# Gated cross-attention with LoRA feed-forward: Q and K of all heads in a phase of their own, by a Strassen scheme, and the rest of the attention in a second phase

## The reference

```
h   = layernorm(x);  xn = rmsnorm(h) * ln_weight
q   = xn @ w_q.T   k = ctx @ w_k.T   v = ctx @ w_v.T        # 1024 x 4096 each, 512 deep
score = q . k + position_bias[head];  masked softmax over 128 keys
attn  = h + (probs . v) @ w_out.T                            # 1024 x 512, 4096 deep
x1  = x + tanh(g_xattn) * attn
y   = layernorm(x1)
out = x1 + tanh(g_ffn) * (y @ base_W.T + base_b + LoRA with a top-8 router)
```

## Time and profile before

| | us |
|---|---|
| median of 3 runs | 947.47 (946.6 to 947.58) |
| the profiled execution | 948.59 |
| its span, first to last instruction | 946.8 |
| PE busy | 920.2 |
| DVE, ACT, POOL busy | 559.4, 437.3, 404.4 |
| DMA | 46.55 MB, mean 49 GB/s |

### The profile page before, as it was taken

The page is one execution under the profiler, slowest core; times in us unless marked ns, Lnnn a source line. Parts: engine busy times, 40 slices in busy tenths (PEclk is TensorE's granted clock), DMA queues, the critical chain, the costliest instruction groups (busy, mean ns, idle before and its releaser), DMA issues.

```text
span 946.8 us, 15495 instructions
## 1 busy us (share of the span) xinstructions
PE 920.2 (97%) x5408; PEld 813.3 (86%) x5408; DVE 559.4 (59%) x953; ACT 437.3 (46%) x1074; POOL 404.4 (43%) x270
## 2 busy tenths in 40 slices
PE   4899999999999999999999999999999999999898
PEld 3788888888888888888888888888888888888787
DVE  7857555556555565556555564556555565657974
ACT  4665444544445454444545354445444454544410
POOL 5345253534445253534534254434525354443432
PEclk9899999999999999999999999999999999999899
DMA  8013020110202020010202020020202020021001
GB/s 289 22 61 136 5 71 23 52 40 3 91 3 91 3 69 25 27 64 3 91 3 91 3 69 22 11 83 3 91 3 87 7 64 28 3 83 56 1 23 67
DMA packets 18929, 46.55 MB, mean 49 GB/s; under 512 B 2528, under 2 KB 7264, under 8 KB 18400
## 3 DMA queue, kind: packets, MB, share of 16 engines
q1 hardware_dynamic: 18912, 46.33, 14.3%
HBM read 44.22 MB, written 2.10 MB: 49 GB/s over the span
## 4 chain that ended last, share of the span: by engine, by line
PE 89%; DVE 6%; ACT 2%; issue 1%; POOL 1%; DMA 1%; SPq 0%; ACTq 0%; DVEq 0%; POOLq 0%
PE QP L1006 6%; PE Ob L1006 6%; PE Vb L1008 6%; PE Vb L1007 6%; PE Vb L1006 6%; PE Ob L1007 6%; PE Ob L1008 6%; PE Kb L1006 6%; PE Kb L1007 6%; PE Kb L1008 6%; PE QP L1008 6%; PE QP L1007 6%; PE Ab L1088 4%; PE Sb L1076 4%; PE QP L1066 3%; PE Sb L1077 2%
## 5 line engine op out<-in xcount | busy, mean ns | idle before, releaser
L336 POOL TENSOR_TENSOR bms<-bm,small_s 128x512 f32<-128x512 f32 x63 | 96.7, 1535 | 208.8 <-ACT small_s L468 208.8
L483 ACT ACTIVATE p_exp<-s_sb,negmax 128x128 f32<-128x128 f32 x256 | 99.8, 391 | 138.2 <-DVE negmax L704 138.2
L1006 PE MATMUL Vb<-v_hi,cT_lo 128*128 128x256 f32 x504 | 143.6, 285 | 9.9 <-DVE cT_lo L638 9.9
L1008 PE MATMUL Vb<-v_hi,cT_hi 128*128 128x256 f32 x504 | 143.8, 285 | 0.0
L1007 PE MATMUL Vb<-v_lo,cT_hi 128*128 128x256 f32 x504 | 143.8, 285 | 0.0
L302 POOL TENSOR_TENSOR qk_lo<-qk_raw,qk_hi 128x1024 fp32r<-128x1024 f32 x32 | 76.8, 2400 | 130.0 <-ACT qk_hi L422 130.0
L422 ACT ACTIVATE P_hl<-QP 128x512 fp32r<-128x512 f32 x64 | 38.4, 599 | 196.9 <-PE QP L1066 196.9
L736 DVE TENSOR_TENSOR acc<-Ob,acc 128x512 f32<-128x512 f32 x120 | 82.2, 685 | 64.7 <-PE Ob L1008 64.7
L1006 PEld LDWEIGHTS Vb<-v_hi,cT_lo 128*128 128x128 f32 x504 | 97.6, 194 | 14.9 <-DVE cT_lo L638 9.9
L1006 PE MATMUL QP<-xT_hi,qk_lo 128*128 128x512 f32 x256 | 104.6, 409 | 0.0
L702 DVE TENSOR_TENSOR s_sb<-Sb,bms 128x512 f32<-128x512 f32 x64 | 44.3, 692 | 101.6 <-POOL bms L336 101.3
(11 more groups left out here) (204 smaller groups left out, 2141.8 us busy)
## 6 DMA issues: line engine op xcount, KB each, us to landing
qk_raw<-wqk SPq DMA_DIRECT2D x32, 512.0 KB, 4.7
v_raw<-wv SPq DMA_DIRECT2D x16, 512.0 KB, 6.0
o_raw<-wo SPq DMA_DIRECT2D x16, 512.0 KB, 3.5
bias_sb<-bias SPq DMA_DIRECT2D x32, 64.0 KB, 1.8
qk_raw<-x SPq DMA_DIRECT2D x2, 1024.0 KB, 5.1
stage<-ctxT SPq DMA_DIRECT2D x4, 256.0 KB, 4.9
acc<-x SPq DMA_DIRECT2D x4, 256.0 KB, 6.8
acc<-x SPq DMA_DIRECT2D x1, 1024.0 KB, 9.9
```

Of the source, the lines that this page charges most:

```text
L336: pool.tensor_tensor(bms[:, :, :], bm[:, :, :], small_s[:, :, :], ALU.add).then_inc(bms_done, 1)
L483: last = act.activation(p_exp[:, i, :], s_sb[:, i, :], ACT.Exp, bias=negmax[:, i:i + 1], accum_out=rowsum[:, i:i + 1])
L1006: pe.matmul(dst, w_lo, m_hi, start=start, stop=False)
L1008: return pe.matmul(dst, w_hi, m_hi, start=False, stop=stop)
```

## The change

Q and K leave the unit's step. They are computed first, in 32 jobs of their own: 16 for K of the head pairs, then 16 for Q. A job is one 2 by 2 block product: the weights of two heads by the two halves of the depth, times the transposed tokens by the same halves and the two halves of the batches. Strassen's scheme (in the Winograd form) makes the four result blocks from seven block products instead of eight. Each product is 2 chunks of the depth by 3 matmuls of 512 columns, so a job is 42 matmuls where the same results took 48.

The seven products need sums. Four sums of weight blocks are made in every job by DVE, 256 wide (`weight_sums`). Four sums of token blocks are made once for the context and once for x. The results are put together partly in PSUM: one bank of `X` takes M1, M6, M7 and M4 one on top of the other, and ACT copies out what stands there after the first three (`snapshot_1` to `snapshot_3`), while DVE adds `Y` (M2) and `Z` (M5, M3) to these. The finished blocks are split into `hi` and `lo` and stored in DRAM (`qk_units`), 512 KB each, four in a job.

The second phase has a unit's scores first, on Q and K that SP has loaded (1 MB a unit, two buffers), then V, output tile, transposes, V, output tile, probabilities times V. Its first output tile goes to `Kb`, the second to `Ob`. The split of the output weights moves from DVE to POOL. What concerns x (norms, transposes, splits) lies between jobs 2 and 16. The feed-forward part is the same work in nearly the same order.

```diff
@@ host: order of the weight blocks, the new tensor in DRAM @@
+    def head_pairs(w):
+        a = heads(w, 1).reshape(G, 2, P, 2, 2 * DH)
+        return np.stack([a[:, 0, :, 0], a[:, 0, :, 1], a[:, 1, :, 1], a[:, 1, :, 0]], axis=2)
...
+    args.append(nc.dram_tensor("qk_units", (UNITS, P, 2, 2 * TH), F32, kind="Internal").ap())
@@ SyncE @@
+            def store(i, n):
+                sp.wait_ge(unit_lo_done[i], n + 1)
+                sp.dma_start(qk_units[4 * (n % G) + i, :, n // G, :], f32(unit_out[:, i, :])).then_inc(st[i], 16)
...
+            for n in range(JOBS + 1):
+                if n + 2 < JOBS:
+                    load_w(n + 2)
...
+                    store(R22, n - 1)
+                if n < JOBS:
+                    store(R11, n)
+                if n > 0:
+                    store(R21, n - 1)
+                    store(R12, n - 1)
+            def load_unit(t, parity):
+                sp.wait_ge(scores_done, t - 1)
+                sp.dma_start(f32(qk[:, parity, :, :]), qk_units[t, :, :, :]).then_inc(ld_qk[parity], 16)
@@ GpSimd, first phase @@
+            def c22_lo(n):
+                pool.wait_ge(unit_hi_done[R22], n + 1)
+                pool.tensor_tensor(unit_half(R22, n, 1), by_batch(C22[:, :]), f32(unit_half(R22, n, 0)),
+                                   ALU.subtract).then_inc(unit_lo_done[R22], 1)
...
+            def first_weights_lo(n):
+                pool.wait_ge(w1_hi, n + 1)
+                pool.tensor_tensor(w_lo[:, n % 2, 0:5, :], w_raw[:, n % 2, 0:5, :], f32(w_hi[:, n % 2, 0:5, :]),
+                                   ALU.subtract).then_inc(w1_lo, 1)
...
+            for n in range(JOBS + 1):
+                if n > 0:
+                    c22_lo(n - 1)
+                if 0 < n < JOBS - 1:
+                    first_weights_lo(n + 1)
+                if n in (3, 4):
+                    rms_root(n - 3)
+                if n in (2, 3):
+                    layernorm_root(n - 2)
+                if n + 1 < JOBS:
+                    last_weights_lo(n + 1)
@@ ScalarE, first phase @@
+            def first_weights_hi(n):
+                act.wait_ge(ld_w[n % 2], 16 * (n // 2 + 1))
+                act.wait_ge(s_add, 4 * n + 3)
+                reached(act, m_done[7], n - 1)
+                high(w_hi[:, n % 2, 0:5, :], w_raw[:, n % 2, 0:5, :], w1_hi)
+            def last_weights_hi(n):
+                act.wait_ge(s_add, 4 * n + 4)
+                reached(act, m_done[3], n - 1)
+                high(w_hi[:, n % 2, 5:7, :], w_raw[:, n % 2, 5:7, :], w2_hi)
+            def snapshot_1(n):
+                act.wait_ge(m_done[1], n + 1)
+                reached(act, c11_done, n)
+                high(U1[:, :], X[n % 2], u1_done)
...
+            for n in range(1, JOBS + 1):
+                snapshot_3(n - 1)
...
+                snapshot_1(n)
+                c22_hi(n - 1)
+                if n + 1 < JOBS:
+                    first_weights_hi(n + 1)
...
+                c11_hi(n)
+                c21_hi(n - 1)
...
+                snapshot_2(n)
...
+                if n + 1 < JOBS:
+                    last_weights_hi(n + 1)
+                c12_hi(n - 1)
...
+                if 5 <= n < 5 + B:
+                    x_evict(n - 5)
+                if n == 9:
+                    x_block_hi(B11)
+                if n == 10:
+                    x_block_hi(B21)
+                if n == 13:
+                    x_block_hi(B22)
+                if n == G - 1:
+                    x_sum_hi(T2, 6)
@@ VectorE, first phase @@
+            def weight_sums(n):
+                w = w_raw[:, n % 2, :, :]
+                dve.wait_ge(ld_w[n % 2], 16 * (n // 2 + 1))
+                dve.tensor_tensor(w[:, S1, :], w[:, A21, :], w[:, A22, :], ALU.add).then_inc(s_add, 1)
+                dve.tensor_tensor(w[:, S3, :], w[:, A11, :], w[:, A21, :], ALU.subtract).then_inc(s_add, 1)
+                dve.wait_ge(s_add, 4 * n + 1)
+                dve.tensor_tensor(w[:, S2, :], w[:, S1, :], w[:, A11, :], ALU.subtract).then_inc(s_add, 1)
+                dve.wait_ge(s_add, 4 * n + 3)
+                dve.tensor_tensor(w[:, S4, :], w[:, A12, :], w[:, S2, :], ALU.subtract).then_inc(s_add, 1)
...
+            def c11(n):
+                dve.wait_ge(m_done[2], n + 1)
+                dve.wait_ge(u1_done, n + 1)
+                reached(dve, unit_lo_done[R11], n)
+                dve.tensor_tensor(C11[:, :], Y, U1[:, :], ALU.add).then_inc(c11_done, 1)
...
+            def unit_lo(i, n, src):
+                dve.wait_ge(unit_hi_done[i], n + 1)
+                low(unit_half(i, n, 1), by_batch(src), unit_half(i, n, 0), unit_lo_done[i])
...
+            for n in range(1, JOBS + 1):
+                c22(n - 1)
...
+                if n + 1 < JOBS:
+                    weight_sums(n + 1)
+                c11(n)
+                unit_lo(R11, n, C11[:, :])
+                if n == G:
+                    x_sum_lo(T2)
+                    x_sum_lo(T1)
+                unit_lo(R21, n - 1, X[(n - 1) % 2])
+                if n == 2:
+                    layernorm_stats(0)
+                if n == 3:
+                    rms_stats(0)
+                    layernorm_stats(1)
+                if n == 4:
+                    rms_stats(1)
...
+                if 4 <= n < 4 + B:
+                    normed(n - 4)
+                if n == 10:
+                    x_block_lo(B11)
+                if n == 11:
+                    x_block_lo(B21)
+                if n == 14:
+                    x_block_lo(B22)
+                    x_sum(T1, B12, B11, 0)
+                    x_sum(T3, B22, B12, 1)
+                if n == 15:
+                    x_sum(T2, B22, B11, 2)
+                    x_sum(T4, B21, B22, 3)
+                if n == 18:
+                    gated_base_b()
+                    router_constants()
+                c12(n - 1)
+                unit_lo(R12, n - 1, C12[:, :])
@@ TensorE @@
+            def blocks(bank, n, a, m_hi, m_lo, fresh, done):
+                for c in range(2):
+                    cols = slice(c * DH, (c + 1) * DH)
+                    hi, lo, first = w_hi[:, n % 2, a, cols], w_lo[:, n % 2, a, cols], fresh and c == 0
+                    pe.matmul(bank, lo, m_hi[:, c, :], start=first, stop=False, skip_group_check=not fresh)
+                    pe.matmul(bank, hi, m_lo[:, c, :], start=False, stop=False, skip_group_check=not fresh)
+                    last = pe.matmul(bank, hi, m_hi[:, c, :], start=False, stop=c == 1, skip_group_check=not fresh)
+                last.then_inc(done, 1)
...
+            def m1(n):
+                pe.wait_ge(w1_lo, n + 1)
+                kept_ready(n, B11)
+                reached(pe, unit_lo_done[R21], n - 1)
+                blocks(X[n % 2], n, A11, *kept(n, B11), True, m_done[1])
+            def m2(n):
+                kept_ready(n, B21)
+                reached(pe, c11_done, n)
+                blocks(Y, n, A12, *kept(n, B21), True, m_done[2])
+            def m3(n):
+                pe.wait_ge(w2_lo, n + 1)
+                kept_ready(n, B22)
+                pe.wait_ge(c22_done, n + 1)
+                blocks(Z[n % 2], n, S4, *kept(n, B22), False, m_done[3])
+            def m4(n):
+                pe.wait_ge(w2_lo, n + 1)
+                sum_ready(n, T4)
+                pe.wait_ge(u3_done, n + 1)
+                blocks(X[n % 2], n, A22, t_hi[:, T4, :, :], t_lo[:, T4, :, :], False, m_done[4])
...
+            def m5(n):
+                sum_ready(n, T1)
+                reached(pe, c12_done, n - 1)
+                blocks(Z[n % 2], n, S1, t_hi[:, T1, :, :], t_lo[:, T1, :, :], True, m_done[5])
+            def m6(n):
+                sum_ready(n, T2)
+                pe.wait_ge(u1_done, n + 1)
+                blocks(X[n % 2], n, S2, t_hi[:, T2, :, :], t_lo[:, T2, :, :], False, m_done[6])
+            def m7(n):
+                sum_ready(n, T3)
+                pe.wait_ge(u2_done, n + 1)
+                blocks(X[n % 2], n, S3, t_hi[:, T3, :, :], t_lo[:, T3, :, :], False, m_done[7])
...
+            def scores(u, g, s):
+                pe.wait_ge(ld_qk[s % 2], 16 * (2 * g + s // 2 + 1))
+                reached(pe, s_done, u)
+                reached(pe, small_s_done, u)
...
-            def q_of(t, g, s):
-                if s < 2:
-                    pe.wait_ge(qk_lo_done, 2 * g + s % 2 + 1)
-                reached(pe, p_lo_done, t - 1)
-                project(QP[:, :], s % 2, 0, xT_hi, xT_lo, s // 2, q_done)
...
-            def k_of(t, g, s):
-                if s < 2:
-                    pe.wait_ge(qk_lo_done, 2 * g + s % 2 + 1)
-                reached(pe, k_lo_done, t)
-                project(Kb[:, :], s % 2, 1, cT_hi, cT_lo, s // 2, k_done)
...
-                q_of(t, g, s)
...
-                if not (first and s == 1):
-                    k_of(t, g, s)
...
-                v_tile(t + 1, g + (s == 3), (s + 1) % 4, 0)
-                if outs:
-                    out_tile(2 * o, og, j)
```

(38 more changed lines are left out.)

1083 lines of the change are left out of this document (575 added, 508 removed).

## The result

The changed kernel takes 961.26 us (median of 4 runs, 959.66 to 961.6), the kernel before 947.32 in the runs beside it: the ratio is 1.0145, with a 95% interval of 1.0128 to 1.0163. It is slower by 1.5%. I had forecast 937.5 us and faster; the direction is wrong. That the range up to 968 holds the time is luck: its upper end was drawn from rivals that didn't come.

What follows compares the result with a forecast made beforehand. The prediction took PE, busy 97% of the span, as the bound. It summed 372.9 us to the first scores, 490 for the second phase and 74 for the tail: 936.9 of span, 937.5 measured time, range 900 to 968.

Steps and rivals of the forecast that it cites:

- The saving: Q and K products: 1344 matmuls for 1536, 192 fewer at 0.231 us, 44.3 us saved; a job 9.69 us on PE.
- with handovers 9.1: First-phase job: the path through ACT, DVE and POOL takes 9.1 us against PE's 9.69, leaving 0.6 us to recover in.
- The start: Loads, context sums and job 0: M7 of job 0 ends near 27.5 us, between 22 and 33.
- The work on x: Jobs 2 to 15: 40 us of norms, copies, splits and sums add to the path; PE waits 26.4 us.
- From K to Q: Job 16: remainders of x's token sums delay M6 and M7, costing 9.3 us.
- Jobs 17 to 31: Jobs without work on x: an ordinary job runs at PE's pace, a period of 9.7 us.
- The second phase: From the first scores to those of unit 63: 490 us, about 25 up to unit 4, then 59 units by 7.88.
- The tail: From the scores of unit 63 to the end: 74 us, against 67.8 before.
- PE bound throughout: Rival for the first phase: DVE's work on x fits into its gaps, waits fall away, 905 us; chance 0.2.
- the port's path of 10.4 in every job: Rival: POOL's next operation goes first at the SBUF port, the path is 10.4 us in every job, 966 us; chance 0.14.
- the unit of the second phase: Rival: POOL's split of 2.35 us lies ahead of `bms`, a unit takes 8.4 us, 968 us; chance 0.08.
- DMA: Rival in the first phase: stores or loads too slow by 0.9 us a job or more, 965 us and over; chance 0.06.

Runs made afterwards that it cites:

- e7_dose: Changed kernel with a norm's two DVE operations repeated on dead data ahead of C12 in jobs 19 to 26: 973.17 us, ratio 1.0274.
- e4_port: Changed kernel with POOL's remainder of 1280 weight columns issued as four shorter instructions: 953.74 us, ratio 1.0065 to the kernel before.
- e9_order2: Changed kernel with e3_gated's and e4_port's edits, work on x moved behind C12's remainder, PE transposes and ACT copies later: 938.1 us, ratio 0.9911.
- e6_hybrid2: Changed kernel with plain products for K, seven products for Q, norm ahead of the result blocks, and e3_gated's spread: 929.53 us, ratio 0.9822.
- e3_gated: Changed kernel with the last group's four acc * tanh + x operations spread behind steps 1, 2 and 3: 958.26 us, ratio 1.0115.
- e5_plain2: Changed kernel without Strassen, 48 plain matmuls a job in the same two phases, norm ahead of the result blocks: 946.63 us, ratio 0.9991.

## Why the prediction was wrong

The forecast span was 936.9, the measured one 959.0. By its own steps:

**The saving.** 192 matmuls at 0.231: right. PE's pace was even 0.227, a job 9.52 instead of 9.69, 5.3 us better over 31 jobs. The path beside it was right in kind. The terms that I listed for it add up to 9.1 without any handover, so "with handovers 9.1" left too much in hand: in e7_dose DVE's 1.6 us more cost 1.23, which is 0.4 us in hand and not 0.6.

**The start** (27.5): M1 of job 1 at 27.9. Right.

**Job 1.** Taken at PE's pace, it took 14.68: 5.2 us lost, a step that the sum didn't have. The sums and remainders of the start were still in DVE's row, beside POOL's long instructions; e4_port took 1.1 of it away, the rest is only argued.

**The work on x** (26.4): 28.0 in jobs 2 to 15, a normed job 11.2 us (the prediction's own terms for eight norms add up to 15.5, not 15.2). Right in size, and in cause as far as e7_dose and e9_order2 show it. It isn't all waiting, as I had put it: PE's idle time there is 18.2 us, and the mean granted clock of 0.98 over 165 us is some 3 more.

**From K to Q** (9.3): 13.0, of which 10.1 are waits: 1.90 on a snapshot, behind the last sums of x, then 5.77 and 2.42 on `t_lo` (3 to 4 us each by my signs). PE went into the long wait at half its clock, behind the waits of job 15 and the 1.90, and came out of it so:

```profile
213.47 0.63 PE L1172 MATMUL Sb<-t_hi,w_hi 128*128 128x512 f32 x1
219.88 0.79 PE L1170 MATMUL Sb<-t_hi,w_lo 128*128 128x512 f32 x1 [5.77 <-DVE t_lo L759]
220.47 0.63 PE L1171 MATMUL Sb<-t_lo,w_hi 128*128 128x512 f32 x1
220.89 0.63 PE L1172 MATMUL Sb<-t_hi,w_hi 128*128 128x512 f32 x1
```

Matmuls start 0.43 us apart there instead of 0.23. The half clock lasts until 223.5, 2 us of the 3.7 by which the turn was dearer. I had counted the waits, not what the clock does around them. The mechanism is right: with the sums made early it is 2.0 us (e6_hybrid2).

**Jobs 17 to 31** (no loss): 3.7, nearly all in the jobs 19, 20 and 24, which lie beside the router constants and the split of V weights (in job 24 two weight sums took 1.58 and 1.51 us instead of 0.42, beside POOL's 2.40 for V and the remainder behind it). With the 0.4 us in hand that e7_dose shows, work of this size in a job must show. In e6_hybrid2 jobs 19 and 24 take 10.75 and 11.19 too.

Together the first scores came at 382.0 instead of 372.9. That alone would have made the span 946.0, still 0.8 under before.

**The second phase** (490): 497.3. The unit was right, 7.855 us for 7.88. The first units took 28.4 instead of 25, and the last two steps up to the scores of unit 63 took 21.1 instead of 15.7, 5.4 us that no step named: 1.0 in the first of them, with the slow `p_norm` beside POOL's split, and 4.4 in the second, with the four operations. The diff doesn't move these four, and I did not look them up. The trace of before has them too, slow as well:

```profile
855.06 5.84 DVE L798 SCALAR_TENSOR_TENSOR acc<-acc,tgate,qk_raw 128x512 f32<-128x512 f32 x4
```

There PE had Q and K of a unit, 5.5 us, to do beside them; after the change it has not. This is the work that hid a cost and went, and e3_gated shows what it was worth: 3.5 us from the scores of unit 61 to those of unit 63.

**The tail** (74): 79.6. The first transposes of y are 16.0 us behind the scores of unit 63 (5.2 before; forecast 13.5), and the base product 32.6 (forecast 25.3), with the clock at 0.67 between 900 and 920 us. The rest is 47.1, as forecast. It is the two-phase order that costs this, not Strassen: e5_plain2 has 79.6. From the first transposes to the base product it was 15.2 us before; I had let it shrink to 11.8 without giving a reason, and it is 16.6. This is the larger part of what the tail's sum lacked.

So the forecast failed by a sum of terms, 9.1 and 7.3 and 5.6, all in one direction. What it lacked was one step: every place where the steady pattern is broken (job 1, the turn to Q, the constants, the first units, the last group) was taken at the steady pace, unless I had seen a reason for more. The margin was 10 us, and these cost 5.2, 3.7, 3.7, 3.4 and 5.4 us more than forecast, before the tail's 5.6. Of the rivals, PE bound throughout is what another order brings nearer (e9_order2); the port's path of 10.4 in every job is out, since most of jobs 17 to 31 run at 9.52, and cutting POOL's long instruction gave back 7.5 us where the rival asked for 29 (the 0.6 us that the prediction gives for a port shared in proportion comes from no row; an operation on 4 numbers alone took 0.16); the unit of the second phase and DMA were as forecast. Slower than before came from none of them, but from many small terms of one sign, for which I had left 0.02.
